# Two causal attentions: first placings between the first visits, warm-up products, and three dense products a step in the last unit

## The chip, the cores and the metric

One core of a Trainium2 chip runs one program. The metric is its time on the device in microseconds, the median of three runs. TensorE (PE) multiplies into PSUM; VectorE (DVE), ScalarE (ACT) and GpSimd (POOL) do the rest of the work, SyncE (SP) issues loads. TensorE runs at one of two clock levels, 1.2 and 2.4 GHz; the profile shows the granted share (0.50 or 1.00) of each stretch.

## The reference

Four layers on 1024 tokens of 256 features: in each an attention of some kind and then a feed-forward part. The change touches two attentions with 16 heads of dimension 16, one in layer 0 and one inside the feed-forward part of layer 1 (without bias and without rotation). Both are

```python
q = rope(proj(Wq, bq))
k = rope(proj(Wk, bk))
v = proj(Wv, bv)
attn = jnp.einsum('bhqd,bhkd->bhqk', q, k) * scale
causal = jnp.triu(jnp.ones((s, s), dtype=bool), k=1)
attn = jnp.where(causal, -jnp.inf, attn)
attn_weights = jax.nn.softmax(attn, axis=-1)
out = jnp.einsum('bhqk,bhkd->bhqd', attn_weights, v)
```

The layer's first line is `x = x + _L0_attn_ref(_layernorm(x, axis=-1), ...)`; the program runs the parts one after another, each in blocks that all engines enter and leave together.

## The kernel before

`small_attention` calls `project` (q, k and v), `attend_causal` and `out_product`. `attend_causal` is what changes. Its tensors carry the prefix `a0h_` in the first attention (about 57 to 278 us of the profile) and `a2h_` in the second (about 1531 to 1753 us).

The work is cut into 8 *units*: a quad of four heads (`Q` 0 to 3) times one half of the 512 queries (`h`), in the order Q0, Q1 for the first half, Q0, Q1 for the second, then Q2 and Q3 likewise. A unit has 4 or 8 *steps*, one for each 128 keys, 48 in all. Step `g` computes the scores of four heads transposed (keys by queries, `scores(g, 0)` and `scores(g, 1)`, L1227, in banks 2 to 4 by turns), ScalarE takes the exponential of each (L1333, `prob`), and `values(g - 1)` multiplies the step before with v into bank 5 (L1249). On the diagonal a mask is added by small bf16 products (L1164).

Ahead of a unit's steps its row maxima must be known. *Visits* (`A`, `maxima(x)`, L1192 and the mask, 48 of them) compute the scores the other way round, and VectorE reduces them (L1366). `M` (`max_rows`, L1211) turns a unit's maxima into rows with eight products, and VectorE adds them to the q tensor (`add_maxima`, L1384, `m_added`); `scores(g, 0)` of a unit's first step waits for that. *Placings* (`P`, `place(i, c)`, L1175 and L1176) spread the heads' 16 rows of q (c = 0) and k (c = 1) over partitions with the 0/1 matrix `put`; a placing is four products of 512 columns, and ScalarE rounds the result into `qt` or `kt` (`rounding`, L1315 and L1317). `D` and `R` are transposes for the denominators behind a unit (L1260, L1269); `ou` is a unit's result copied by ScalarE (L1345).

`A`, `M`, `P`, `D` and `R` share a ring of two PSUM pairs (`ring`, `spare`, `wait_spare`): the use number in `uses` picks the pair, and a use waits until the second last one was read. The order of all this is written out by hand: `head` comes ahead of the steps, `after[g]` lists what stands in step `g`, and `visits_by(g)` says how many visits are done by step `g`. On TensorE a step is

```python
scores(g, 0)
others(events[:1])
scores(g, 1)
events = events[1:]
others(events)
if 0 < g <= len(steps):
    values(g - 1)
others([e for e in after[g] if e[0] in "DR"])
```

Before the first placing VectorE clears `put` (L1353), GpSimd fills six pieces of it from the identity (L1147), then `one_row`, the masks and the negative identity (`made`), ScalarE makes the high part of the chunks of `qk` (`high`, L1305) and VectorE the low part (L1357). The head's order is: four placings, visits 0 to 3, four placings, `M` of unit 0, visits 4 and 5.

## Time and profile before

| | us |
|---|---|
| median of 3 runs | 2941.66 |
| lowest and highest run | 2924.04 and 2943.62 |
| profiled execution | 2920.74 |
| its span (the profile's) | 2919.0 |
| mean granted clock of TensorE | 0.911 |
| busy: PE, DVE, ACT, POOL | 2560.7, 1620.0, 1261.6, 1276.2 |

The profile gives the span of one execution. A busy TensorE is not TensorE at its peak, since matmuls overlap and their ends are modelled. A product whose operands are both plain fp32 stands there as two records. A line's number is a line of the kernel; `x8` behind a row is the number of instructions merged in it.

### The profile page before, as it was taken

The numbers are of one execution on the slowest core, as the hardware profiler recorded it, in microseconds if no ns is written. First come the engines' busy times: TensorE is split into PE (matmuls) and PEld (weight loads), VectorE is DVE, ScalarE is ACT, GpSimd is POOL, SyncE is SP. The second block draws the span as 40 slices with busy tenths as digits, with TensorE's granted clock in tenths as the row PEclk, the third lists the DMA queues.
The fourth block names the chain that finished last, engine by engine and source line by source line (L and its number), as shares of the span: only waits on it lengthen the run. The fifth ranks groups of instructions, "written<-read, shape, count | busy, mean of one in ns | idle before, by whom it ended". The sixth has DMA issues, their size and how long they took to land. (4 is left out here: it accounts for less than half of the span.)

```text
span 2919.0 us, 41072 instructions
## 1 busy us (share of the span) xinstructions
PE 2560.7 (88%) x14559; PEld 1710.4 (59%) x14562; DVE 1620.0 (55%) x2144; ACT 1261.6 (43%) x2127; POOL 1276.2 (44%) x1116
## 2 busy tenths in 40 slices
PE   5887799784999999999867886979999988997698
PEld 4443677562444444444554434768888866775576
DVE  3662355475666666664335543467777744554555
ACT  3464233371555555555323562245655542333232
POOL 3000344282888888888502002245454522442143
PEclk7696899996999999999975897989999997999799
DMA  1000111102111011010100001010000001110011
GB/s 48 1 1 8 36 44 49 45 24 81 37 35 37 23 37 37 15 30 1 29 11 5 1 1 41 19 56 19 26 30 19 19 4 34 49 44 19 24 44 41
DMA packets 40142, 82.17 MB, mean 28 GB/s; under 512 B 7856, under 2 KB 21424, under 8 KB 39472
## 3 DMA queue, kind: packets, MB, share of 16 engines
q1 hardware_dynamic: 37392, 76.25, 9.3%
q10 hardware_dynamic: 2592, 3.82, 0.4%
q8 instruction: 98, 1.61, 0.2%
q14 instruction: 60, 0.49, 0.1%
HBM read 60.12 MB, written 3.15 MB: 22 GB/s over the span
## 5 line engine op out<-in xcount | busy, mean ns | idle before, releaser
L1836 DVE TENSOR_REDUCE a1h_mseg<-bank 128x2 f32<-128x1024 f32 x256 | 302.4, 1222 | 185.0 <-PE bank L1601 176.8
L1763 ACT ACTIVATE a1h_prob<-bank 128x512 f32<-128x512 f32 x440 | 246.9, 598 | 189.9 <-PE bank L1657 103.1
L1585 POOL TENSOR_TENSOR a_qk<-a_qk,a1h_prob 128x512 f32<-128x512 f32 x230 | 298.7, 1330 | 48.9 <-ACT a1h_prob L1763 48.9
L63 POOL TENSOR_TENSOR f_wh<-f_raw,ones_r 128x768 fp32r<-128x768 f32 (+1 forms) x74 | 111.3, 1503 | 408.1 <-PE bank L402 371.2
L391 PE MATMUL bank<-x_norm_h,f_wh 128*128 128x512 f32 x592 | 241.6, 408 | 10.1 <-POOL f_wl L359 9.6
L391 PE MATMUL bank<-x_norm_l,f_wh 128*128 128x512 f32 x592 | 237.1, 401 | 0.0
L391 PE MATMUL bank<-x_norm_h,f_wl 128*128 128x512 f32 x592 | 236.5, 399 | 0.0
L600 DVE SCALAR_TENSOR_TENSOR f_tf<-bank,f_bias,f_sg 128x512 f32<-128x512 f32 x148 | 111.0, 751 | 201.6 <-PE bank L391 181.1
L1670 PE MATMUL bank<-a1h_prob,a_v 128*64 128x512 f32 x880 | 215.0, 603 | 0.0
L1655 PE MATMUL bank<-a1h_ql,a1h_k 128*128 128x512 f32 x512 | 202.1, 395 | 0.0
L488 ACT ACTIVATE f_hhi<-f_hf 128x512 fp32r<-128x512 f32 x124 | 78.3, 632 | 271.9 <-DVE f_hf L608 271.7
L614 DVE TENSOR_TENSOR f_hlo<-f_hf,f_hhi 128x512 fp32r<-128x512 f32 x124 | 112.1, 905 | 82.7 <-ACT f_hhi L488 82.4
L477 ACT ACTIVATE f_sg<-bank,f_bias 128x512 f32<-128x512 f32 x148 | 101.8, 688 | 128.1 <-PE bank L391 128.1
L1585 POOL TENSOR_TENSOR x_norm<-x_norm,a1h_prob 128x512 f32<-128x512 f32 x104 | 134.7, 1330 | 24.7 <-ACT a1h_prob L1763 24.6
L391 PEld LDWEIGHTS bank<-x_norm_h,f_wh 128*128 128x128 f32 x592 | 113.5, 192 | 52.0 <-issue 13.3
L359 POOL TENSOR_TENSOR f_wl<-f_raw,f_wh 128x768 fp32r<-128x768 f32 (+1 forms) x74 | 127.6, 1725 | 5.9
L402 PE MATMUL bank<-f_hhi,f_wh 128*128 128x512 f32 x296 | 118.4, 400 | 13.3 <-DVE f_hlo L614 13.3
L391 PEld LDWEIGHTS bank<-x_norm_l,f_wh 128*128 128x128 f32 x592 | 113.2, 191 | 27.8
L391 PEld LDWEIGHTS bank<-x_norm_h,f_wl 128*128 128x128 f32 x592 | 113.5, 192 | 24.8
L1654 PE MATMUL bank<-x_norm_h,a1h_kn 128*128 128x512 f32 x256 | 119.4, 467 | 4.1 <-DVE a1h_k L1824 2.2
L2616 POOL TENSOR_TENSOR l2a_rope<-l2a_rope,l2a_tab 128x512 f32<-128x512 f32 x64 | 81.2, 1276 | 90.1 <-ACT l2a_rope L2493 89.1
L1654 PE MATMUL bank<-x_norm_l,a1h_kn 128*128 128x512 f32 x256 | 118.5, 463 | 0.9
(564 smaller groups left out, 6189.8 us busy)
## 6 DMA issues: line engine op xcount, KB each, us to landing
f_raw<-in_l_w_dram SPq DMA_DIRECT2D x66, 385.0 KB, 3.1
a1h_st_q<-a_qk SPq DMA_DIRECT2D x128, 128.0 KB, 2.4
a_qk<-l_keys SPq DMA_DIRECT2D x32, 128.0 KB, 2.8
l2a_qkraw<-in_l2a_wqk_dram SPq DMA_DIRECT2D x32, 128.0 KB, 2.1
l2a_vraw<-in_l2a_wvg_dram SPq DMA_DIRECT2D x8, 512.0 KB, 3.8
f_raw<-in_l_w_dram SPq DMA_DIRECT2D x8, 449.0 KB, 3.4
a1p_raw<-in_l1a_w_dram SPq DMA_DIRECT2D x20, 128.0 KB, 2.0
l_keys<-a_qk SPq DMA_DIRECT2D x4, 512.0 KB, 4.0
```

The source lines that it names most:

```text
L63: return pool.tensor_tensor(dst, src, one.to_broadcast(list(src.shape)), ALU.mult)
L359: pool.tensor_tensor(wl[:, slot, :], raw[:, slot, 0:B], wh[:, slot, :].bitcast(F32), ALU.subtract).then_inc(w_split, 1)
L391: mm = pe.matmul(out[:, :], w[:, slot, c0:c0 + P], x, start=n == 0, stop=n == 3 * n_k - 1)
L402: mm = pe.matmul(acc[m][h][:, :], w[:, slot, c0:c0 + P], x[:, h, :], start=begin and n == 0, stop=False, skip_group_check=True)
L600: dve.scalar_tensor_tensor(tf[:, h, :], up[h][:, :], bias[:, slot, 1:2], sg[:, h, :], ALU.add, ALU.mult).then_inc(t_ready, 1)
L614: dve.tensor_tensor(hl[:, h, :], src[:, h, :], hh[:, h, :].bitcast(F32), ALU.subtract).then_inc(hl_ready, 1)
L1585: pool.tensor_tensor(out, first, slot_of[t % NP], ALU.add).then_inc(sum_done, 1)
L1654: pe.matmul(bank[:, :], kn[:, G % 2, a, keys], QA[n % 2][:, a, half(h)], start=True, stop=False)
L1655: mm = pe.matmul(bank[:, :], k1[:, a, keys], ql[:, n % 2, a, half(h)], start=False, stop=lo >= hi)
L1670: pe.matmul(core.bank[5][64 * a:64 * a + 64, :], v[:, kb, 2 * (n // 4) + a, :], slot_of[t % NP], start=kb == 0, stop=kb == TB - 1, skip_gr ...
L1763: act.activation(slot_of[t % NP], core.bank[2 + t % 3][:, :], ACT.Exp, scale=scale).then_inc(p_ready, 1)
L1836: dve.tensor_reduce(mseg[:, :, qb, s], spare(("A", n, k))[:, :, :], AX.X, ALU.max).then_inc(a_read, 1)
```

## The change

- The head becomes: four placings, then visits 0 to 3 with one of the other four placings behind each, then `M` of unit 0. Visits 4 and 5 leave the head and stand in step 0. `visits_by` is one visit lower at each step.
- All eight placings of the head (`FIRST`) leave the ring: they use the pairs 1 and 2 by turns (banks 2 to 5, of the scores and the values) and wait for `rounded` of the second last. A unit's first scores wait for `rounded` 8.
- GpSimd makes the first two kinds of `put` (three pieces), ScalarE the other two (three `Copy` activations, `keys_made`), behind the first two `high`. The first placing waits for three pieces, the next three for ScalarE's.
- Ahead of the first placing TensorE makes four products of the identity with a half of `qk` (plain fp32, 512 columns) into bank 5. Their result is not used.
- In visits 0 to 3 each pair of heads gets its mask (`mask_pair`) right behind its product; before, both pairs' masks came behind both products.
- In `after[g]` visits now come first, then `M` and `P`. So between the two score pairs of a step stands a visit where there is one, and `M` comes behind the second pair.
- `high` of chunks 2 and 3 moves from steps 0 and 1 to steps 8 and 9.
- In steps 40 to 47 TensorE makes three more products of 512 columns (`zero_r` with `kt`, fp32r, into bank 1) behind `values`. Their result is not used.

```diff
@@ -1043,12 +1043,11 @@
 
     def visits_by(g):
 
-        return min(len(visits), 6 + g + 1 + min(4, max(0, g - 1)))
+        return min(len(visits), (6, 7, 8, 10, 12, 14, 16)[g] if g < 7 else g + 10)
 
     after = [[] for _ in range(len(steps) + 6)]
-    head = [("A", x) for x in range(4)] + [("M", 0)] + [("A", x) for x in range(4, 6)]
     for g in range(len(steps)):
-        for x in range(visits_by(g - 1) if g else 6, visits_by(g)):
+        for x in range(visits_by(g - 1) if g else 4, visits_by(g)):
             after[g].append(("A", x))
             for w in range(1, len(UNITS)):
                 if LAST_VISIT[w] == x:
@@ -1056,19 +1055,23 @@
     for w in range(len(UNITS)):
         after[LAST_STEP[w] + 3].append(("D", w))
         after[LAST_STEP[w] + 5].append(("R", w))
-    head = [("P", i, c) for i in range(2) for c in range(2)] + head[:4]
-    head += [("P", i, c) for i in range(2, 4) for c in range(2)] + [("M", 0)] + [("A", x) for x in range(4, 6)]
+    head = [("P", i, c) for i in range(2) for c in range(2)]
+    for x in range(4):
+        head += [("A", x), ("P", 2 + x // 2, x % 2)]
+    head.append(("M", 0))
+    FIRST = [e for e in head if e[0] == "P"]
     for Q in range(2, QUADS):
         x = min(x for x, vi in enumerate(visits) if UNITS[vi[0]][0] == Q)
         first = min(g for g in range(len(steps)) if ("A", x) in after[g])
         for i in range(4):
             after[first - 3 + min(i, 2)].append(("P", 2 * Q + i // 2, i % 2))
     placed = [e for e in head if e[0] == "P"] + [e for es in after for e in es if e[0] == "P"]
-    after = [[e for e in es if e[0] in "APM"] + [e for e in es if e[0] in "DR"] for es in after]
+    after = [[e for k in ("A", "MP", "DR") for e in es if e[0] in k] for es in after]
     order = head + [e for es in after for e in es]
     uses = []
     for e in order:
-        uses += [("A", e[1], 0), ("A", e[1], 1)] if e[0] == "A" else [e]
+        if e not in FIRST:
+            uses += [("A", e[1], 0), ("A", e[1], 1)] if e[0] == "A" else [e]
     use = {e: u for u, e in enumerate(uses)}
 
     def width(g):
@@ -1082,7 +1085,8 @@
         sem = lambda n: nc.alloc_semaphore(f"{name}_{n}")
         sb = lambda n, shape, dt=F32: ctx.enter_context(nc.sbuf_tensor(f"{name}_{n}", shape, dt))
         c_in, made, hi, lo = sem("c_in"), sem("made"), sem("hi"), (sem("lo0"), sem("lo1"))
-        rounded, cleared = sem("rounded"), sem("cleared")
+        rounded, cleared, keys_made = sem("rounded"), sem("cleared"), sem("keys_made")
+        first_placed = sem("first_placed")
         a_ready, a_read, m_steps, m_added = sem("a_ready"), sem("a_read"), sem("m_steps"), sem("m_added")
         s_ready, p_ready, av_done = sem("s_ready"), sem("p_ready"), sem("av_done")
         ou_done, r_steps, rx_done, on_done = sem("ou"), sem("r_steps"), sem("rx"), sem("on")
@@ -1108,10 +1112,16 @@
 
         def spare(key):
 
+            if key in FIRST:
+                return core.pair[1 + FIRST.index(key) % 2]
             return ring[use[key] % 2]
 
         def wait_spare(pe, key):
 
+            if key in FIRST:
+                if FIRST.index(key) >= 2:
+                    pe.wait_ge(rounded, FIRST.index(key) - 1)
+                return
             u = use[key] - 2
             if u < 0:
                 return
@@ -1141,7 +1151,7 @@
         def _(pool):
             pool.wait_ge(cleared, 1)
             columns = core.ident[:, :].rearrange("p (n v u) -> p v u n", v=4, u=2)
-            for kind, places in enumerate(PLACES):
+            for kind, places in enumerate(PLACES[0:2]):
                 rows = put[:, kind, :, :].rearrange("p v (u n) -> p v u n", u=2)
                 for s in places:
                     pool.tensor_scalar(rows[:, :, :, 16 * s:16 * s + 16], columns, 1.0, None,
@@ -1175,7 +1185,7 @@
                     pe.matmul(ps[:, t, :], put[:, 2 * c, i % 4, :], HI[g][:, c, half(t)], start=True, stop=False)
                     mm = pe.matmul(ps[:, t, :], put[:, 2 * c + 1, i % 4, :], LO[g][:, c, half(t)], start=False,
                                    stop=True)
-                mm.then_inc(a_ready, 1)
+                mm.then_inc(first_placed if ("P", i, c) in FIRST else a_ready, 1)
 
             def maxima(x):
 
@@ -1194,13 +1204,19 @@
                                        tile_position=(64 * u, 0))
                     if not diag:
                         mm.then_inc(a_ready, 1)
-                if diag:
+                    elif x < 4:
+                        mask_pair(x, p, n)
+                if diag and x >= 4:
                     for p in range(2):
-                        ps = spare(("A", x, p))
-                        for c in range(2):
-                            for u in range(2):
-                                mm = mask(pe, ps[:, u, n - P + 64 * c:n - P + 64 * c + 64], 0, c, u)
-                        mm.then_inc(a_ready, 1)
+                        mask_pair(x, p, n)
+
+            def mask_pair(x, p, n):
+
+                ps = spare(("A", x, p))
+                for c in range(2):
+                    for u in range(2):
+                        mm = mask(pe, ps[:, u, n - P + 64 * c:n - P + 64 * c + 64], 0, c, u)
+                mm.then_inc(a_ready, 1)
 
             def max_rows(w):
 
@@ -1219,6 +1235,7 @@
                 c0, n, diag = width(g)
                 if kb == 0 and p == 0:
                     pe.wait_ge(m_added, w + 1)
+                    pe.wait_ge(rounded, len(FIRST))
                 if 4 * g + 2 * p >= 2:
                     pe.wait_ge(p_ready, 4 * g + 2 * p - 1)
                 for u in range(2):
@@ -1283,9 +1300,13 @@
                     else:
                         inverse(x)
 
-            pe.wait_ge(made, 7)
-            others(head[:4])
-            pe.wait_ge(made, 8)
+            for x in range(4):
+                pe.matmul(core.bank[5][:, :], core.ident[:, :], qk[:, 0, half(x % 2)], start=True, stop=True)
+            pe.wait_ge(made, 3)
+            others(head[:1])
+            pe.wait_ge(keys_made, 3)
+            others(head[1:4])
+            pe.wait_ge(made, 5)
             others(head[4:])
             for g in range(len(steps) + 6):
                 events = [e for e in after[g] if e[0] in "APM"]
@@ -1297,6 +1318,9 @@
                 others(events)
                 if 0 < g <= len(steps):
                     values(g - 1)
+                if LAST_STEP[-2] < g < len(steps):
+                    for _ in range(3):
+                        pe.matmul(ring[0][:, 1, :], core.zero_r[:, :], kt[:, 0, half(0)], start=True, stop=True)
                 others([e for e in after[g] if e[0] in "DR"])
 
         @block.scalar
@@ -1308,7 +1332,10 @@
                 Q = i // 2
                 if Q >= SLOTS and i % 2 == 0:
                     act.wait_ge(s_ready, 4 * (LAST_STEP[UNITS.index((Q - SLOTS, 1))] + 1))
-                act.wait_ge(a_ready, use["P", i, c] + 1)
+                if ("P", i, c) in FIRST:
+                    act.wait_ge(first_placed, FIRST.index(("P", i, c)) + 1)
+                else:
+                    act.wait_ge(a_ready, use["P", i, c] + 1)
                 dst = (qt, kt)[c][:, 2 * (Q % SLOTS) + i % 2, :]
                 src = spare(("P", i, c)).rearrange("p h q -> p (h q)")
                 if c == 0:
@@ -1318,7 +1345,13 @@
 
             high(0)
             high(1)
-            act.wait_ge(made, 7)
+            act.wait_ge(cleared, 1)
+            columns = core.ident[:, :].rearrange("p (n v u) -> p v u n", v=4, u=2)
+            for kind, places in enumerate(PLACES[2:4]):
+                rows = put[:, 2 + kind, :, :].rearrange("p v (u n) -> p v u n", u=2)
+                for s in places:
+                    act.activation(rows[:, :, :, 16 * s:16 * s + 16], columns, ACT.Copy).then_inc(keys_made, 1)
+            act.wait_ge(made, 4)
             for kind, i, *c in head:
                 if kind == "P":
                     rounding(i, c[0])
@@ -1332,8 +1365,8 @@
                         act.wait_ge(s_ready, t + 1)
                         act.activation(prob[:, t % NP, 0:n], core.bank[2 + t % 3][:, 0:n], ACT.Exp,
                                        scale=scale).then_inc(p_ready, 1)
-                if g < 2:
-                    high(g + 2)
+                if 8 <= g < 10:
+                    high(g - 6)
                 for e in after[g]:
                     if e[0] == "P":
                         rounding(e[1], e[2])
@@ -1370,7 +1403,7 @@
                     if w >= 2:
                         dve.wait_ge(m_added, w - 1)
                     elif w == 0:
-                        dve.wait_ge(made, 10)
+                        dve.wait_ge(made, 7)
                     out = mpos[:, w % 2, :, 48:P:64].rearrange("p (a b) u -> p a u b", a=2)
                     got = mseg[:, w % 2, :, :, :].rearrange("p (a u) b s -> p a u b s", a=2)
                     for p in range(2):
```

## Rows read from the trace of the kernel before

**Rows 1.** Windows: us, length; busy (count) of PE, PEld, DVE, ACT, POOL; PEclk; DMA.

```profile
57.50:90.20 32.70, 19.16 (x118) 13.21 (x118) 12.72 (x17) 11.61 (x12) 10.24 (x10) 0.73 0.04 11
90.20:132.70 42.50, 36.68 (x274) 19.51 (x276) 26.97 (x34) 15.02 (x36) 4.71 (x2) 0.58 0.00 1
132.70:241.40 108.70, 94.33 (x932) 47.68 (x930) 69.19 (x91) 69.59 (x146) 0.00 (x0) 0.99 0.00 1
241.40:272.70 31.30, 25.58 (x142) 8.85 (x142) 1.12 (x3) 15.77 (x35) 0.00 (x0) 0.53 0.01 1
...
1531.70:1566.60 34.90, 21.90 (x120) 15.52 (x120) 13.03 (x18) 11.80 (x12) 10.23 (x10) 0.63 0.04 10
1566.60:1609.80 43.20, 37.91 (x274) 20.06 (x276) 26.66 (x33) 15.13 (x37) 4.72 (x2) 0.54 0.00 1
1609.80:1723.30 113.50, 99.66 (x932) 50.43 (x928) 69.29 (x91) 69.59 (x147) 0.00 (x0) 0.93 0.01 1
1723.30:1747.90 24.60, 18.88 (x142) 6.81 (x142) 1.12 (x3) 15.70 (x35) 0.00 (x0) 0.79 0.00 1
```

**Rows 2.** Timeline, first head: start, us, engine, line, operation [idle before, releaser].

```profile
58.84 5.36 POOL L1147 TENSOR_SCALAR a0h_put<-ident 128x128 fp32r<-128x128 f32 x6 [8.04 <-DVE a0h_put L1353]
...
64.41 0.80 PE L1175 MATMUL bank<-x_norm_h,a0h_put 128*128 128x512 f32 x1 [7.68 <-POOL a0h_one_row L1149]
...
70.64 1.11 ACT L1317 ACTIVATE a0h_kt<-bank,a0h_one_row 128x1024 fp32r<-128x1024 f32 x1
...
71.85 0.44 PE L1192 MATMUL bank<-a0h_kt,a0h_qt 64*128 64x128 f32 x4 [1.25 <-ACT a0h_kt L1317]
...
72.40 0.76 DVE L1366 TENSOR_REDUCE a0h_mseg<-bank 128x2 f32<-128x256 f32 x2 [11.16 <-PE bank L1164]
...
73.71 1.29 DVE L1366 TENSOR_REDUCE a0h_mseg<-bank 128x2 f32<-128x512 f32 x2 [0.56 <-PE bank L1164]
...
78.47 2.36 DVE L1366 TENSOR_REDUCE a0h_mseg<-bank 128x2 f32<-128x1024 f32 x2 [1.02 <-PE bank L1164]
...
79.75 0.79 PE L1175 MATMUL bank<-x_norm_h,a0h_put 128*128 128x512 f32 x1 [1.21 <-DVE a0h_mseg L1366]
...
85.58 1.00 PE L1211 MATMUL bank<-a0h_nident,a0h_mpos 128*128 128x128 f32 x8
...
86.62 1.22 DVE L1384 TENSOR_TENSOR a0h_qt<-a0h_qt,bank 128x1024 fp32r<-128x1024 f32 x1 [5.51 <-PE bank L1211]
...
90.20 1.08 ACT L1333 ACTIVATE a0h_prob<-bank 128x512 f32<-128x512 f32 x2 [2.01 <-PE bank L1164]
```

**Rows 3.** Timeline of GpSimd alone, 60.5 to 62.3.

```profile
60.37 1.99 POOL L1147 TENSOR_SCALAR a0h_put<-ident 128x128 fp32r<-128x128 f32 x2
```

**Rows 4.** Timeline of TensorE's weight loads, 11.5 to 13, in the first norm.

```profile
11.86 0.19 PEld L128 LDWEIGHTS bank<-x_resid,mean_w 128*128 128x128 f32 x1 [0.24 <-issue]
12.29 0.19 PEld L128 LDWEIGHTS bank<-x_resid,mean_w 128*128 128x128 f32 x1 [0.24 <-issue]
```

**Rows 5.** Windows (columns as in rows 1) ahead of the first placing.

```profile
58.00:60.00 2.00, 0.00 (x0) 0.00 (x0) 2.00 (x3) 1.49 (x2) 1.16 (x1) 0.76 0.50 115
```

**Rows 6.** Timeline, first head again, two placing products at full clock.

```profile
83.16 0.40 PE L1175 MATMUL bank<-x_norm_h,a0h_put 128*128 128x512 f32 x1
...
83.40 0.39 PE L1176 MATMUL bank<-x_norm_l,a0h_put 128*128 128x512 f32 x1
```

**Rows 7.** Timeline of ScalarE, step 38 of the first attention.

```profile
238.47 0.66 ACT L1333 ACTIVATE a0h_prob<-bank 128x256 f32<-128x256 f32 x2 [1.87 <-PE bank L1164]
```

**Rows 8.** Timeline, step 44 of the second attention: the first scores of the step.

```profile
1737.37 0.49 PE L1227 MATMUL bank<-a2h_qt,a2h_kt 64*128 64x512 f32 x2
```

**Rows 9.** Timeline of ScalarE, last unit of the second attention.

```profile
1735.29 1.09 ACT L1333 ACTIVATE a2h_prob<-bank 128x512 f32<-128x512 f32 x2 [2.49 <-PE bank L1227]
...
1738.04 1.08 ACT L1333 ACTIVATE a2h_prob<-bank 128x512 f32<-128x512 f32 x2
...
1747.85 0.60 ACT L1345 ACTIVATE a2h_ou<-bank 128x512 f32<-128x512 f32 x1 [0.55 <-PE bank L1249]
```

## The prediction

> **What bounds the kernel now.** The granted clock comes first. Over the whole span its mean is 0.91, but the table of stretches [rows 1] shows where it is low, and two of the places are the two causal attentions that the change touches. I cut each into five stretches: the head (block start to the first exponential), steps 0 to 7, the middle (steps 8 to 39), the last unit (steps 40 to 47), and the end, which the change does not touch. The first attention spends 32.7, 42.5, 108.7 and 31.3 us, the second 34.9, 43.2, 113.5 and 24.6. So 431 of 2919 us can move and nothing else can. TensorE was busy 36.68 of 42.5 us in steps 0 to 7 at a clock of 0.58, and 94.33 of 108.7 us in the middle at 0.99. The last unit is the most telling pair: the same 142 records of TensorE took 31.3 us at a clock of 0.53 and 24.6 us at 0.79. There the visits have run out, TensorE alternates with ScalarE's exponentials, and the clock falls to its lower level (1.2 of 2.4 GHz).
>
> The timeline of the first head [rows 2] is a chain. GpSimd makes six pieces of the placing matrix; TensorE's first placing starts at 64.41, 6.9 us after the block began at 57.5; four placings and their roundings end at 71.75 (70.64 + 1.11); the first visit's product starts at 71.85 and the fourth visit's reduce ends at 80.83 (78.47 + 2.36); only from 79.75 do the other four placings run; the row maxima are added at 86.62, and the first exponential starts at 90.20, behind visits 4 and 5.
>
> **The head, part by part.** (a) GpSimd makes three of the six pieces before the first placing, ScalarE the other three. The six took 5.36 us [rows 2]; the first ran alone to 60.37, and the next two ended at 62.36 [rows 3]. The first placing moves from 64.41 to 62.4, 2.0 us earlier. ScalarE rounds the first two chunks of `qk` and then has nothing until a placing is ready; three copies of 128 columns, an eighth of the 1.1 us rounding's 1024 each, hide behind GpSimd (were each a whole rounding, they would end near 62.9 and still be in time for the second placing).
>
> (b) Four full fp32 products are put ahead on TensorE, which waits for nothing then. The nearest fp32 product is that of the mean, two records each; at the full clock their weight loads are 0.43 us apart [rows 4], so a product is 0.86 us and four are 3.4: 57.5 to 60.95, inside the wait. At half clock throughout they are 6.9 us and end at 64.4, where the placing starts today: even then they cost only what (a) gained. What they buy is the clock: without them it fell between 58 and 60 (0.76 in that stretch [rows 5]) with TensorE idle since the value products, and the first placings ran at half speed.
>
> (c) The four placings. At full clock their products are 0.24 us apart [rows 6], 0.96 for the four of one placing, so ScalarE's roundings (1.0 and 1.1 us) lead: 62.4 + 1.05 + four roundings of 1.1 each with their wait gives 67.8. At half clock it is 62.4 + 4 × 1.7 + 1.2 = 70.4. TensorE still idles 1.4 us between the products and the first placing, so I take 68.3.
>
> (d) Visits 0 to 3 with one placing behind each. Today 9.0 us from first product to last reduce, of which VectorE's four pairs of reduces are about 6.2 (0.76, 1.29, a pair between, 2.36) [rows 2]. The placings no longer use the ring of two PSUM pairs and go into TensorE's gaps, and each half of a visit now gets its mask directly. I leave 8.7 us for this, then the eight products of the row maxima (1.0), the addition (1.2), and 1.4 for scores and hand-overs: 12.3 us. The first exponential: 68.3 + 12.3 = 80.6, against 90.20: **-9.6**. The second attention's head has the same work and took 34.9 us [rows 1]; 23.1 us again gives **-11.8**. At half clock throughout, a placing is 1.7 us, a visit about 1.4, the row maxima 2: about 17 us from a start at 70.4, hence 87.4, gains of only 2.8 and 5.0.
>
> (e) Visits 4 and 5 are not gone. They now sit in step 0; the reduces of such a pair of visits are 0.76 and 1.29 [rows 2]: **+2.0** each attention (between 0 and the 2.5 of a slow clock).
>
> **The middle.** The count of visits done by each step falls by one, so each unit's row maxima (`M`) come in the last step of the unit before (units 1, 2, 3, 6, 7), behind that step's visit. Today `M` stands between the two score pairs of a step, and the exponentials then wait 1.87 us [rows 7]. That stall goes, but its place is taken: after `M` come the addition (1.2) and the first scores of the new unit, and where a 512-wide visit stands in front of it VectorE does 2.4 us of reduces first; `values` of that step covers 0.6 to 1 us. I count five boundaries at +0.4 and two freed steps at -0.5: **+1.0** each attention. The bounds: a full 1.9 us won at each of two freed steps (-4), or an addition and a 1.2 us half visit fully exposed at five (+12). Two 1.06 us roundings `high` move from steps 0 and 1 to 8 and 9; TensorE is the later one there about half of the time: **+0.8** (0 to 2.1). Later `P`s move by one step with their visits: nothing.
>
> **The last unit.** Three products of 512 columns a step in eight steps. At the full clock 0.7 us a step [rows 6]; at the lower 1.3. They stand between `values` and the next step's scores, and those follow one another without a gap in the stretch of the second attention's last unit that ran at full clock (values end, scores start at 1737.37 [rows 8]), so they are on the path: TensorE leads by 0.2 to 0.5 us there, and only the places with ScalarE's extra copies hide some. Without them, the unit at full clock is 2.75 us for a step (1735.29 to 1738.04) and 9.8 for the last four (1738.04 to 1747.85) [rows 9]: 4 × 2.75 + 0.7 for a transpose + 9.8 = 21.5. Eight times 0.7 less 0.6 hidden: 26.5. That is **-4.8** against 31.3 and **+1.9** against 24.6. It rests on the clock staying up: TensorE's share rises from about two thirds to four fifths. The Trainium skill ("TensorE: Matmul & The Clock Gate", section "Back-to-back issue gap") gives about 131 ns for a 512-column product in a real stream. By its figure the 48 products would cost 6.3 us instead of 11.3 (48 x 0.235), and the sum would come out 5 us lower, at 2920; the rows here show 0.24, and I keep them.
>
> **Sum.** First attention: -9.6 + 2.0 + 1.0 + 0.8 - 4.8 = -10.6. Second: -11.8 + 2.0 + 1.0 + 0.8 + 1.9 = -6.1. Together -16.7 us. Against the profiled execution, 2920.74 us, that is 2904; the three runs shown have a median of 2941.66, 21 us above it, so in their terms it is 2925.
>
> **Rivals.**
> 1. *The dense products do not lift the clock.* The last unit stays at the lower level and is PE-bound: 31.3 + 8 × 1.28 = 41.5 us in both, +10.2 and +16.9 instead of -4.8 and +1.9. Sum +13.3: 2955, slower than before. For it: at the lower level TensorE was already busy 25.58 of 31.3 us [rows 1] and the clock did not rise. Against: a packed 1.3 us a step closes most of what was idle. It decides when over half of the unit's steps run at 0.5. 10%.
> 2. *Steps 0 to 7 turn warm.* The head ends at the full clock; if it held, VectorE would lead with 27 us of reduces and additions (26.97 busy today [rows 1]) and the stretch would be near 33 instead of 42.5: 10 us less in each, 2905. Against: these steps have small products and long waits for reduces, and the clock fell there both times. 17%.
> 3. *The head stays cold*, because of the 1.4 us gap and thin visits: 6.8 us lost in each, 2939. 13%.
> 4. *The row maxima become the wait.* If at five boundaries in each attention the addition and half a visit (2.4 us) are exposed and the freed stalls give nothing: +24 - 2 = +22, 2947, again slower. It shows in exponentials waiting over 4 us at the first step of a unit. 10%.
>
> My forecast itself has 50%. The median of three runs of this kernel moves over 20 us (2924 to 2944), so about 1% is what can be told from no change. The range 2897 to 2950 takes in rivals 2, 3 and 4 and leaves out the first and the tails. Faster by over 1% (below 2912) is most of rival 2 and the low end of my own: 0.20. Slower by over 1% needs rivals 1 and 4 together: 0.04. Within 1%: 0.76.
>
> **What would show it.** First placing 4.9 us after the block start; four mean-like products ahead of it with a clock of 1.0; first exponential 23 us after the start (rival 3: 30); steps 0 to 7 near 44 us (rival 2: 33); no 1.87 us wait inside a step, but one of 2 to 3 us at the first step of units 3, 6 and 7; the last unit 26 to 27 us in both at a clock over 0.9 (rival 1: 41 at 0.5). The rest of the kernel, some 2490 us, must not move; if it does by more than 5 us, the difference isn't the change.

## The result and the profile after

| | before | changed kernel |
|---|---|---|
| median of 20 runs each, us | 2942.47 | 2925.01 |
| lowest and highest | 2918.15 and 2957.85 | 2916.04 and 2933.75 |
| ratio, 95% interval | | 0.9952 [0.9934, 0.9969] |
| profiled execution, us | 2920.74 | 2933.75 |

The changed kernel is 0.5% faster, within the 1% that was called no change, and lands on the 2925 that was forecast. Its runs lie closer together (18 us against 40).

The stretches of the two attentions, cut as in [rows 1] (start, length, busy time and count of PE, PEld, DVE, ACT, POOL, granted clock, DMA share, GB/s): head, steps 0 to 7, steps 8 to 39, last unit.

```profile
58.40:81.20 22.80, 17.55 (x104) 10.61 (x106) 11.37 (x14) 12.63 (x14) 8.41 (x7) 0.97 0.06 16
81.20:122.90 41.70, 34.84 (x288) 18.58 (x288) 27.47 (x34) 13.35 (x34) 0.00 (x0) 0.62 0.00 1
122.90:236.70 113.80, 99.94 (x944) 51.61 (x942) 70.38 (x93) 71.49 (x148) 4.75 (x2) 0.92 0.01 1
236.70:271.70 35.00, 29.72 (x166) 12.59 (x166) 1.12 (x3) 15.81 (x34) 0.00 (x0) 0.70 0.00 1
1535.60:1558.20 22.60, 17.32 (x104) 10.54 (x106) 11.42 (x14) 12.69 (x14) 8.41 (x7) 0.99 0.06 15
1558.20:1600.60 42.40, 35.06 (x290) 19.89 (x288) 27.43 (x34) 13.35 (x34) 0.00 (x0) 0.62 0.00 1
1600.60:1714.30 113.70, 99.68 (x944) 51.15 (x942) 70.38 (x93) 71.53 (x149) 4.74 (x2) 0.92 0.01 1
1714.30:1746.80 32.50, 27.25 (x166) 11.65 (x166) 1.11 (x3) 15.79 (x35) 0.00 (x0) 0.78 0.00 1
```

Against [rows 1]: the heads fell from 32.7 and 34.9 us to 22.8 and 22.6. Steps 0 to 7 stayed (42.5 and 43.2 to 41.7 and 42.4). The middle went from 108.7 to 113.8 in the first attention and stayed at 113.5 in the second. The last unit grew from 31.3 to 35.0 and from 24.6 to 32.5, with 24 more records of TensorE. With the transposes behind it an attention went from 220.1 and 221.0 us to 217.8 and 215.6.

So in these two executions the attentions gained 7.7 us, while the medians differ by 17.5. The profiled execution of the changed kernel is the slowest of its 20 runs. What lies outside the attentions, where nothing was changed, took 2478 us in the profiled execution of before and 2499 in that of the changed kernel; over all 14 profiled executions of this study it lies between these two values. The prediction said that the rest must not move by more than 5 us, or else the difference isn't the change. It moved by 21, so the spans of these two executions can't be compared; what follows goes by stretches and by medians. An execution of before that was profiled later (below) took 233.9 and 234.0 us for its attentions. The mean over both profiles of before is 227.3 an attention, and the changed kernel's 216.7 is 10.6 less: 21 us for the two. That is near the medians' difference, but it is an estimate: the two executions of before (2920.7 and 2959.2 us) lie near the two ends of its runs, there is one of the changed kernel, and what lies outside the attentions is left out of it. The first profile of before, on which the prediction rests, is of an execution near the fast end of its runs.

The head, in the timeline (compare [rows 2]):

```profile
58.34 3.67 PE L1304 MATMUL bank<-a_on,ident 128*128 128x512 f32 x8 [0.79 <-PEq L821]
...
59.67 3.52 POOL L1157 TENSOR_SCALAR a0h_put<-ident 128x128 fp32r<-128x128 f32 x3 [7.80 <-DVE a0h_put L1386]
...
60.24 1.08 ACT L1353 ACTIVATE a0h_put<-ident 128x128 fp32r<-128x128 f32 x3
...
63.25 0.50 PE L1185 MATMUL bank<-x_norm_h,a0h_put 128*128 128x512 f32 x1 [1.23 <-POOL a0h_put L1157]
...
63.59 0.39 PE L1186 MATMUL bank<-x_norm_l,a0h_put 128*128 128x512 f32 x1
...
63.82 0.39 PE L1185 MATMUL bank<-x_norm_h,a0h_put 128*128 128x512 f32 x1
...
67.87 1.11 ACT L1344 ACTIVATE a0h_kt<-bank,a0h_one_row 128x1024 fp32r<-128x1024 f32 x1
...
81.23 1.09 ACT L1366 ACTIVATE a0h_prob<-bank 128x512 f32<-128x512 f32 x2 [2.06 <-PE bank L1174]
```

The four fp32 products take 3.67 us and end at 62.0; GpSimd has three pieces to make, ScalarE's three take 1.08 us beside them. The first placing starts 4.9 us after the block start, with products 0.23 us apart as in [rows 6]; the last rounding of the first four ends at 68.98, the first exponential starts at 81.23, 22.9 us after the block start.

The row maxima of unit 7, in step 39:

```profile
231.19 0.33 PE L1244 MATMUL bank<-a0h_qt,a0h_kt 64*128 64x128 f32 x2
...
232.97 1.39 PE L1227 MATMUL bank<-a0h_nident,a0h_mpos 128*128 128x128 f32 x8 [1.38 <-DVE a0h_mpos L1410]
...
234.29 0.47 PE L1244 MATMUL bank<-a0h_qt,a0h_kt 64*128 64x128 f32 x2
...
234.40 1.22 DVE L1417 TENSOR_TENSOR a0h_qt<-a0h_qt,bank 128x1024 fp32r<-128x1024 f32 x1 [1.57 <-PE bank L1227]
...
234.99 0.45 ACT L1366 ACTIVATE a0h_prob<-bank 128x128 f32<-128x128 f32 x2 [2.86 <-PE bank L1174]
...
235.84 0.79 PE L1244 MATMUL bank<-a0h_qt,a0h_kt 64*128 64x512 f32 x2
```

TensorE's first score pair of step 39 ends at 231.5. All visits are done by step 38, so none stands in this step, and the one event that there is, `M`, comes between the two score pairs; behind the second pair it would stand only in a step with a visit. It waits for the last visit's reduces until 232.97 (1.38 us idle). The second pair follows at 234.29, and ScalarE's exponentials wait 2.86 us for it (2.66 in the second attention), where they waited 1.87 in step 38 before ([rows 7]). The addition runs from 234.40 and unit 7's first scores start at 235.84. The same place by windows:

```profile
231.00:233.00 2.00, 0.62 (x11) 0.34 (x7) 1.79 (x4) 0.67 (x3) 0.00 (x0) 1.00 0.00 0
233.00:235.00 2.00, 2.00 (x18) 1.79 (x22) 0.60 (x1) 0.01 (x1) 0.00 (x0) 0.65 0.03 8
235.00:237.00 2.00, 1.63 (x10) 0.31 (x6) 0.62 (x1) 0.71 (x3) 0.00 (x0) 0.50 0.00 0
```

The clock is at its upper level through the wait and falls at 233.6, within the second stretch (0.65), while the row maxima run. It stays at 0.50 for 24 us. In the second attention it falls at 1711.6, 0.9 us after the row maxima began, and stays low for 17 us. One step's dense products at each level, in TensorE's timeline:

```profile
242.53 1.93 PE L1266 MATMUL bank<-a0h_prob,a_v 128*32 128x512 f32 x8
244.39 1.65 PE L1323 MATMUL bank<-a0h_kt,zero_r 128*128 128x512 f32 x3
245.97 0.80 PE L1244 MATMUL bank<-a0h_qt,a0h_kt 64*128 64x512 f32 x2
...
263.67 1.07 PE L1266 MATMUL bank<-a0h_prob,a_v 128*32 128x512 f32 x8
264.66 0.96 PE L1323 MATMUL bank<-a0h_kt,zero_r 128*128 128x512 f32 x3
265.55 0.39 PE L1244 MATMUL bank<-a0h_qt,a0h_kt 64*128 64x256 f32 x2
```

At the lower level `values` start at 242.53, the three products at 244.39, and the next scores follow at 245.97: 1.58 us. At the upper level 264.66 to 265.55: 0.89 us.

### The profile page after: what moved, and what is told of

Read it like the earlier page. It is cut to its first block and busy times, and to the rows that moved or that the text cites. A ratio compares the mean times of both kernels' runs of the same rounds, so it can differ in the third digit from the quotient of the medians.

```text
span 2932.0 us, 41205 instructions
## 1 busy us (share of the span) xinstructions
PE 2584.7 (88%) x14626; PEld 1727.4 (59%) x14626; DVE 1621.4 (55%) x2144; ACT 1264.1 (43%) x2133; POOL 1273.0 (43%) x1110
## 5 line engine op out<-in xcount | busy, mean ns | idle before, releaser
L391 PEld LDWEIGHTS bank<-x_norm_h,f_wh 128*128 128x128 f32 x592 | 114.3, 193 | 52.1 <-issue 13.4
L391 PEld LDWEIGHTS bank<-x_norm_l,f_wh 128*128 128x128 f32 x592 | 114.3, 193 | 28.1
L1687 PE MATMUL bank<-x_norm_h,a1h_kn 128*128 128x512 f32 x256 | 119.4, 466 | 5.3 <-DVE a1h_k L1857 3.5
L1366 ACT ACTIVATE a0h_prob<-bank 128x512 f32<-128x512 f32 (+3 forms) x192 | 83.8, 489 | 85.3 <-PE bank L1174 56.4
```

The costliest lines, as they stand in the source:

```text
L391: mm = pe.matmul(out[:, :], w[:, slot, c0:c0 + P], x, start=n == 0, stop=n == 3 * n_k - 1)
L1687: pe.matmul(bank[:, :], kn[:, G % 2, a, keys], QA[n % 2][:, a, half(h)], start=True, stop=False)
```

## The experiments

Stretches of each kernel's profiled execution, first and second attention, in us. "Sum" is both attentions, including the transposes at the end.

| kernel | head | steps 0 to 7 | steps 8 to 39 | last unit | sum | median, us | ratio to before [95%] |
|---|---|---|---|---|---|---|---|
| before | 32.7, 34.8 | 42.5, 43.2 | 108.7, 113.5 | 31.2, 24.6 | 441.1 | 2942.5 | |
| before again | 34.8, 34.8 | 43.2, 43.2 | 119.4, 119.4 | 31.6, 31.6 | 467.9 | one run, 2959.2 | |
| changed | 22.9, 22.6 | 41.7, 42.4 | 113.8, 113.7 | 35.0, 32.5 | 433.4 | 2925.0 | 0.9952 [0.9934, 0.9969] |
| e1 no dense | 22.9, 22.6 | 41.4, 42.6 | 114.3, 113.7 | 23.0, 23.0 | 412.9 | 2913.8 | 0.9917 [0.9881, 0.9953] |
| e2 dense only | 32.7, 34.7 | 42.5, 43.2 | 111.5, 113.4 | 27.3, 29.9 | 444.2 | 2944.0 | 1.0014 [0.9985, 1.0042] |
| e3 no warm-up | 23.9, 24.1 | 42.8, 40.7 | 113.5, 114.3 | 30.5, 37.6 | 436.0 | 2929.9 | 0.9974 [0.9949, 0.9999] |
| e4 fill the wait | 22.5, 22.9 | 42.6, 43.2 | 114.8, 115.6 | 22.6, 23.9 | 416.7 | 2907.3 | 0.9894 [0.9846, 0.9943] |
| e5 old order | 22.5, 22.5 | 41.2, 41.2 | 116.3, 116.2 | 26.4, 26.4 | 420.9 | 2921.8 | 0.9940 [0.9907, 0.9973] |
| e6 visits earlier | 22.5, 22.5 | 45.6, 45.6 | 111.7, 111.8 | 27.5, 27.5 | 423.4 | 2907.1 | 0.9875 [0.9807, 0.9943] |
| e7 six dense | 22.9, 22.9 | 41.1, 41.7 | 112.9, 113.8 | 34.9, 36.8 | 435.0 | one run, 2925.6 | |
| e9 old head order | 25.8, 24.9 | 38.5, 43.1 | 114.4, 115.2 | 27.9, 26.4 | 424.6 | 2913.8 | 0.9961 [0.9937, 0.9985] |
| e10 fill all waits | 22.7, 22.9 | 45.7, 45.6 | 120.7, 116.4 | 23.9, 23.9 | 429.8 | 2917.9 | 0.9971 [0.9955, 0.9987] |
| e11 roundings early | 22.9, 22.8 | 41.4, 41.6 | 112.4, 112.9 | 24.9, 24.9 | 413.4 | 2908.2 | 0.9940 [0.9919, 0.9962] |
| e12 both | 22.5, 22.7 | 41.9, 44.1 | 112.8, 115.2 | 31.2, 28.1 | 427.6 | 2911.8 | 0.9921 [0.9897, 0.9944] |

Kernels of one group (e1 to e4; e5 to e7 and before again; e9 to e11; e12) ran on one chip each, against the kernel before on the same chip, whose median there was 2939.4, 2938.5, 2927.7 and 2936.6. Ratios can be compared across groups, medians less so.

**Without the dense products (e1).**

```diff
-                if LAST_STEP[-2] < g < len(steps):
-                    for _ in range(3):
-                        pe.matmul(ring[0][:, 1, :], core.zero_r[:, :], kt[:, 0, half(0)], start=True, stop=True)
```

> The changed kernel without the three products a step in the last unit; everything else stays. In the changed kernel the last unit took 35.0 and 32.5 us. Theory A (the clock falls because the row maxima M7 now wait for a visit's reduce directly before the unit, with TensorE idle; the dense products only lengthen each step, 1.4 us at the lower clock and 0.9 at the higher): the clock still falls ahead of the last unit, its low steps take 4.1 us again instead of 5.7, and the unit takes 29 to 33 us if the clock stays low, 25 to 27 if it comes back in the middle; the kernel is 2 to 12 us faster than the changed one. Theory B (the dense products pay, because they alone bring the clock back in the unit): the unit stays low to its end and takes over 33 us, and the kernel is slower than the changed one.

Windows of the two last units:

```profile
237.30:260.30 23.00, 17.54 (x142) 6.43 (x142) 1.11 (x3) 15.67 (x34) 0.00 (x0) 0.85 0.01 1
1704.90:1728.00 23.10, 17.55 (x142) 6.42 (x142) 1.12 (x3) 15.72 (x35) 0.00 (x0) 0.85 0.00 1
```

Where the clock came back in the first (windows, and TensorE's `values` behind them):

```profile
243.00:244.30 1.30, 1.30 (x6) 0.29 (x2) 0.00 (x0) 0.01 (x1) 0.00 (x0) 0.50 0.00 0
244.30:246.00 1.70, 0.95 (x8) 0.34 (x10) 0.00 (x0) 1.33 (x3) 0.00 (x0) 1.00 0.00 0
...
245.59 1.07 PE L1266 MATMUL bank<-a0h_prob,a_v 128*32 128x512 f32 x8
```

23.0 and 23.0 us, below every figure that either theory gave. The clock fell at 237.5 in the first attention, as the unit began, and 3 us ahead of the unit in the second, so theory A's place for it is about right. It came back after 7 and 10 us, without dense products. What brought it back isn't shown. By the ratios e1 gains 0.35% (10 us) more than the changed kernel, though the two intervals overlap at their ends; in the profiles the two attentions are 20.5 us shorter. Theory B falls: the clock comes back without the dense products. Against before, e1 is 0.83% faster: that is what all of the change but the dense products is worth.

**Only the dense products (e2).** The same three lines added to the kernel before.

> The kernel before with only the three dense products a step in steps 40 to 47 added; M7 stays one step earlier, in step 38. Before: 31.2 and 24.6 us. Theory A (where M7 stands decides on the clock; dense products then hold it): with M7 in its old place the dense products keep the clock up and the unit takes 26 to 27 us in both, the kernel 0 to 4 us faster than before. Theory B (the clock falls at the thin last steps of unit 6 anyway and dense products are too few to bring it back soon): 32 to 38 us in both, the kernel 5 to 15 us slower than before.

```profile
245.70:273.00 27.30, 22.00 (x166) 9.96 (x166) 1.11 (x3) 15.81 (x35) 0.00 (x0) 1.00 0.01 2
1727.90:1757.80 29.90, 24.65 (x166) 10.86 (x166) 1.12 (x3) 15.78 (x35) 0.00 (x0) 0.89 0.00 1
```

In the first attention the unit ran wholly at the upper level and took 27.3 us; this is the one execution in which the forecast's condition held, and there its 26.5 is nearly right. In the second the clock was low for 7 us at the unit's start: 29.9. Theory A nearly holds for the first (it said 26 to 27), neither for the second. The kernel as a whole isn't to be told from before (1.0014). The dense products don't keep the clock from falling. And even where it stayed up, 27.3 us is more than the 23.0 to 24.9 that the unit took without the products in e1 and e11, with the clock low for 7 to 12 of them: at 0.9 us a step the products cost more than the clock they were to save.

**Without the warm-up products (e3).**

```diff
-            for x in range(4):
-                pe.matmul(core.bank[5][:, :], core.ident[:, :], qk[:, 0, half(x % 2)], start=True, stop=True)
```

> The changed kernel without the four fp32 products ahead of the first placing. Heads in the changed kernel: 22.9 and 22.6 us at a clock of 0.97 and 0.99. Theory A (the clock in the head is theirs): the clock falls before the first placing, the placings run at 0.43 us a product instead of 0.24, and the heads take 26 to 30 us; the kernel is 6 to 14 us slower than the changed one. Theory B (the new order with placings between visits does it alone, the chain of roundings and reduces leads at either clock): the heads take 23 to 25 us and the kernel is within 4 us of the changed one.

Window of the first head:

```profile
58.70:82.60 23.90, 14.99 (x98) 10.23 (x98) 11.38 (x14) 12.64 (x14) 8.39 (x7) 0.86 0.06 15
```

and of its timeline, the first three products of a placing:

```profile
63.56 0.79 PE L1185 MATMUL bank<-x_norm_h,a0h_put 128*128 128x512 f32 x1 [5.68 <-POOL a0h_put L1157]
64.15 0.63 PE L1186 MATMUL bank<-x_norm_l,a0h_put 128*128 128x512 f32 x1
64.57 0.63 PE L1185 MATMUL bank<-x_norm_h,a0h_put 128*128 128x512 f32 x1
```

The clock is low at the first placing (products 0.42 us apart), as theory A says, and the head's mean clock falls from 0.97 to 0.86. But the head takes 23.9 us (24.1 in the second), 1.0 and 1.5 more than with them. Theory B's figure for the heads holds: in these profiles the four products are worth 2.5 us of the 22 that the two heads gained. Only the first placings ran slowly here: the clock was back at 66.8, 3 us after the first of them began. So what a head costs that stays cold throughout isn't shown. The median is 5 us higher than the changed kernel's, but the two intervals overlap; the last units (30.5 and 37.6) together took only 0.6 us more.

**Fill the wait ahead of the row maxima (e4).** e1, and in `max_rows`:

```diff
                 wait_spare(pe, ("M", w))
-                pe.wait_ge(m_steps, w + 1)
                 ps = spare(("M", w))
+                if w >= 6:
+                    for _ in range(6):
+                        pe.matmul(ps[:, 1, :], core.zero_r[:, :], kt[:, 0, half(0)], start=True, stop=True)
+                pe.wait_ge(m_steps, w + 1)
```

> The changed kernel without the dense products of the steps, but with six products of 512 columns in the wait for the reduces ahead of the row maxima of units 6 and 7 (into the PSUM pair that those use next). Theory A (the idle time of TensorE ahead of M7 is what lowers the clock): the clock stays at its upper level through unit 6's start and into unit 7, the six products (1.4 us) hide in the wait, and the last unit takes 21.5 to 25 us; the kernel is 8 to 16 us faster than the changed one. Theory B (thin scores and values lower it a few steps later anyway): the clock falls within unit 7 and it takes 27 to 31 us, no more than 5 us from the run without dense products.

```profile
237.00:259.60 22.60, 16.74 (x142) 6.17 (x142) 1.12 (x3) 15.58 (x34) 0.00 (x0) 0.92 0.00 1
1700.90:1724.80 23.90, 17.96 (x142) 6.48 (x142) 1.12 (x3) 15.62 (x35) 0.00 (x0) 0.86 0.00 0
```

and of its timeline, the fill in step 39 and the row maxima behind it:

```profile
232.56 1.66 PE L1227 MATMUL bank<-a0h_kt,zero_r 128*128 128x512 f32 x6
234.06 1.00 PE L1230 MATMUL bank<-a0h_nident,a0h_mpos 128*128 128x128 f32 x8
```

Six products fit the wait: step 39 took 4.24 us, against 4.28 and 5.05 in e1. The clock still fell, 3 to 4 us after the unit's first exponential, for 3 and 7 us (e1: with that exponential and 3 us ahead of it). 22.6 and 23.9 us are in theory A's range, yet e1 without the fill has 23.0 and 23.0. At unit 6 the fill didn't fit: step 31 took 6.28 against 5.18 and 5.93. So the idle wait isn't the cause by itself. Theory B's cause, the thin steps around it, fits but wasn't tested by itself. The ratio (0.9894) isn't separated from e1's (0.9917).

**The old order in a step (e5).** e1 with `after` sorted as before, `M` ahead of the visit.

```diff
-    after = [[e for k in ("A", "MP", "DR") for e in es if e[0] in k] for es in after]
+    after = [[e for e in es if e[0] in "APM"] + [e for e in es if e[0] in "DR"] for es in after]
```

> The changed kernel without the dense products and with the old order inside a step (the row maxima ahead of the visit, between the two score pairs). Reference is the same kernel with the new order: middle (steps 8 to 39) 114.3 and 113.7 us, 2914 us. Theory A (the wait for the reduces is the same wherever the row maxima stand, it only moves): middle 112 to 117 us in both, the kernel within 5 us. Theory B (the new order is what made the middle longer than before's 108.7 and 113.5, since the visit's half reduce and the addition now lie ahead of the unit's first scores): middle under 110 us in both, 8 us or more faster.

The middle took 116.3 and 116.2 us, 2.0 and 2.5 more than in e1, and steps 0 to 7 41.2. Its clock was 0.90 there against 0.93 and 0.92, so the 2 us can be the clock's and not the order's. Theory A holds for the middle, B falls: the new order isn't what makes the middle longer than 108.7. Its ratio, 0.9940, overlaps e1's, though the medians are 8 us apart on different chips.

**A visit earlier (e6).** e1 with the old `visits_by`.

```diff
-        return min(len(visits), (6, 7, 8, 10, 12, 14, 16)[g] if g < 7 else g + 10)
+        return min(len(visits), 6 + g + 1 + min(4, max(0, g - 1)))
```

> The changed kernel without the dense products and with one visit more done by each step, as before (three visits in step 0), so that the row maxima come a step earlier. Theory A (row maxima directly ahead of their unit are the cause of the 5 us step before units 3, 6 and 7 and of the clock falling there): the middle shrinks by 3 to 6 us in each attention, step 0 grows by 2 us, the kernel is 2 to 8 us faster than 2914. Theory B (each unit pays one wait of about 3 us anyway, wherever it stands): the middle stays within 2 us, steps 0 to 7 too, and the kernel within 3 us of 2914.

```profile
79.90:125.40 45.50, 39.43 (x298) 21.69 (x298) 28.38 (x36) 13.33 (x34) 0.00 (x0) 0.54 0.00 1
125.40:237.20 111.80, 100.58 (x932) 50.87 (x930) 69.39 (x91) 71.59 (x149) 4.73 (x2) 0.91 0.01 1
237.20:264.70 27.50, 21.59 (x142) 7.43 (x142) 1.11 (x3) 15.70 (x35) 0.00 (x0) 0.69 0.00 1
```

The middle shrank by 2.6 and 1.9 us (theory A said 3 to 6). Steps 0 to 7 grew by 3 to 4; step 0 alone, with one visit more and the clock low in both kernels, took 5.3 us instead of 3.1, the 2 that A said. And the last unit began without a wait (steps 38 and 39 5.5 us together instead of 6.5 to 7.3), but the clock fell in it all the same, 3 us after its start. In the profile the sum is 10 us worse than e1's; in the medians it is the best ratio, 0.9875, of only four runs (the profiled one is the slowest of them) and with an interval that holds e1's ratio. It isn't settled by these runs which is better.

**Six dense products a step (e7).** The changed kernel with `range(6)` for `range(3)`.

> The changed kernel with six dense products a step instead of three in the last unit. It prices one product and tells whether more of them hold the clock. Theory A (they lie on the path, 0.30 us each at the upper clock, 0.53 at the lower, and do not decide when the clock falls, because it falls ahead of them): steps at the upper clock take 2.75 + 1.8 = 4.5 us and 2.10 + 1.8 = 3.9, the last unit 38 to 46 us. Theory B (three are too few, six fill TensorE and bring the clock back within a few us): the low stretch in the unit is under 7 us in both attentions and the unit takes under 37 us.

```profile
236.60:271.40 34.80, 29.57 (x190) 15.49 (x190) 1.11 (x3) 15.77 (x34) 0.00 (x0) 0.92 0.00 1
1712.80:1749.70 36.90, 31.55 (x190) 16.18 (x190) 1.11 (x3) 15.85 (x35) 0.00 (x0) 0.86 0.00 0
```

and of its timeline, step 46:

```profile
266.04 1.65 PE L1323 MATMUL bank<-a0h_kt,zero_r 128*128 128x512 f32 x6
```

Steps 45 and 46 took 4.12 and 3.68 us where the changed kernel took 3.43 and 3.00 and e1 2.54 and 2.10. So the first three cost 0.90 us and the next three 0.69: 0.23 us for a product and 0.2 once a step. The clock was low for 7 us around the first unit's start and 14 us around the second's; neither theory's figures fit throughout. With three products the low stretches were 24 and 17 us here but 0 and 7 in e2, so one execution doesn't show that six shorten them; the units took 34.9 and 36.8 us against 35.0 and 32.5.

**The kernel before once more (e8).**

> The kernel before once more, unchanged, for a second profile. In the first its last units took 31.2 and 24.6 us and its heads 32.7 and 34.8. Theory A (the stretches of the attentions repeat within 1 us except where the clock's turns fall otherwise: steps 0 to 7, the last unit): heads again 32 to 35 us, the last units anywhere from 23 to 32. Theory B (each stretch has its own fixed time): all ten stretches within 1 us of the first profile.

Windows of its first attention:

```profile
59.30:94.00 34.70, 21.77 (x120) 15.45 (x120) 12.94 (x18) 11.68 (x11) 10.25 (x10) 0.62 0.04 10
94.00:137.20 43.20, 37.90 (x274) 20.05 (x276) 26.74 (x33) 15.14 (x36) 4.75 (x2) 0.54 0.00 1
137.20:256.70 119.50, 106.69 (x932) 53.44 (x930) 69.49 (x91) 69.84 (x147) 0.00 (x0) 0.86 0.01 1
256.70:288.30 31.60, 26.15 (x142) 9.03 (x142) 1.12 (x3) 15.79 (x35) 0.00 (x0) 0.50 0.00 1
```

The middle took 119.5 us at a clock of 0.86, where the first profile has 108.7 at 0.99 ([rows 1]); the last unit ran wholly at 0.50. Both attentions took 234 us. Theory A is right in kind but too narrow: the middle isn't fixed either.

**The second placings behind the visits again (e9).** e1, with

```diff
-    for x in range(4):
-        head += [("A", x), ("P", 2 + x // 2, x % 2)]
+    head += [("A", x) for x in range(4)] + [("P", 2 + x // 2, x % 2) for x in range(4)]
```

> The changed kernel without the dense products, and with the head's second four placings behind visits 0 to 3 again instead of between them; they still use the scores' banks, three pieces still come from ScalarE, the four fp32 products stay. Heads of the same kernel with the new order: 22.9 and 22.6 us. Theory A (the placings between the visits are the largest part of the 10 to 12 us that the head gained: they took 5.7 us behind the visits, of which half was hidden): the heads take 25.5 to 28 us and the kernel is 5 to 10 us slower than 2914. Theory B (leaving the ring is enough, since the placings then run while VectorE still reduces visit 3): the heads take 23 to 25 us, the kernel within 4 us.

```profile
59.60:85.40 25.80, 20.70 (x106) 13.39 (x106) 11.40 (x14) 12.55 (x14) 8.39 (x7) 0.80 0.05 14
1526.90:1551.80 24.90, 19.85 (x106) 12.35 (x106) 11.42 (x14) 12.71 (x15) 8.40 (x7) 0.86 0.05 14
```

25.8 and 24.9 us: 2.9 and 2.3 more. Theory A's range holds the first; the second lies in theory B's. The clock fell within these heads (to 0.80 and 0.86, against 0.98 and 0.99 in e1), so a part of the 2.9 and 2.3 is the clock's, and the two aren't taken apart. The interleaving is the largest single part of the head that was tried, of two. Steps 0 to 2 came out 3 us shorter in the first attention and 1 in the second; in the first the clock was up there, in e1 it was down.

**Fill all waits (e10).** e4 with the fill at units 1 to 7 (four products at 1 and 2).

> Dense products of 512 columns, with an unused result, in TensorE's wait ahead of the row maxima of every unit but the first (four for units 1 and 2, six for 3 to 7), and none in the steps of the last unit. With the fill at units 6 and 7 alone the last units took 22.6 and 23.9 us, the middle 114.8 and 115.6, steps 0 to 7 42.6 and 43.2, the kernel 2907. Theory A (each low stretch begins in such a wait, so filling it keeps the clock): the middle drops to 105 to 110 us at a clock over 0.96, steps 0 to 7 to 36 to 41, the kernel to 2885 to 2900. Theory B (low stretches come from the thin steps around too, and the fill costs where it does not fit the wait): each stretch stays within 2 us or grows, and the kernel is at 2905 to 2920.

Against e1, steps 0 to 7 grew by 3 to 4 us and the middle by 3 to 6. The middle's clock was 0.93 and 0.97 (e1: 0.93 and 0.92), that of steps 0 to 7 0.60 and 0.65 (0.64 and 0.58). Theory B. In steps 3, 7, 15, 19 and 23 the wait is shorter than the fill, and the dense products stand on the path.

**The two roundings early (e11).** e1 with `high` back in steps 0 and 1.

```diff
-                if 8 <= g < 10:
-                    high(g - 6)
+                if g < 2:
+                    high(g + 2)
```

> The changed kernel without the dense products and with the two roundings of the second half of qk back in steps 0 and 1 (from 8 and 9). Theory A (ScalarE is the later engine there about half of the time, as forecast: they cost 0.8 us an attention at steps 8 and 9): steps 8 and 9 together take 0.5 to 2 us less, steps 0 and 1 at most 0.5 more, the kernel 0 to 4 us faster than 2914. Theory B (TensorE leads in steps 8 and 9, the move cost nothing): steps 8 and 9 within 0.3 us of the same steps at the same clock level.

Steps 8 and 9 took 6.39 and 6.94 us instead of 6.82 and 7.17; steps 0 and 1 took 7.76 and 7.77 in both kernels. So the move costs 0.2 to 0.4 us an attention in these executions, between the two theories. The clock of steps 8 and 9 was lower in e11 than in e1 (0.73 against 1.00, 0.60 against 0.67), so it can be more.

**The combination (e12).** e11 with the fill of e4 at unit 7 alone.

> The changed kernel without the dense products of the steps, with the two roundings of the second half of qk in steps 0 and 1, and with six dense products in the wait ahead of the row maxima of unit 7 alone. Theory A (only the fill that fits its wait pays; it delays the clock's fall into the last unit): steps 38 and 39 stay at 2.3 and 4.3 us, the last units take 22.5 to 25 us, the middle 112 to 114, the attentions 203 to 208 each, the kernel 2900 to 2910 and 0.7 to 1.3% below before. Theory B (when the clock turns is chance, the fill does nothing): the last units anywhere between 23 and 28 us and the kernel within 4 us of 2908 to 2914.

```profile
234.40:265.60 31.20, 25.34 (x142) 8.79 (x142) 1.12 (x3) 15.69 (x34) 0.00 (x0) 0.54 0.00 1
```

The fill fitted (steps 38 and 39: 2.25 and 4.23 us), and the clock fell 2 us into the unit and stayed low to its end in the first attention: 31.2 us. With the same fill ahead of the same unit it was low for 3 and 7 us in e4. Theory A's range is missed; B's range for the last units is too (31.2 and 28.1), its median is met. Of the versions tried, e1, e4, e6 and e12 are all faster than before by 0.8 to 1.25%, and e1 is the plainest: the changed kernel without the step's dense products.

## Why the prediction was right, and where it wasn't

**The head: right in size, partly in cause.** Forecast -9.6 and -11.8 us, measured -9.8 and -12.2 (-11.9 and -12.2 against before again). The first placing came 4.9 us after the block start as forecast. Step (b), that the four products buy the clock, is right about the clock (0.97 instead of 0.86), and without them the heads took 1.0 to 1.5 us more (e3). The rival of a cold head (30 us) asked for the lower level throughout; that occurred in no run, so its size stays untested. Interleaving gives at most 2.3 to 2.9. The rest, some 6 to 8 us, lies with the earlier first placing, visits 4 and 5 behind the first exponential, the placings outside the ring, and the masks; these were not taken apart.

**Steps 0 to 7: wrong by 3 us an attention.** Forecast +2.0 for the two visits, measured -0.8 and -0.8. To price a visit by its reduces fits (e6's third visit in step 0 has 1.82 us of them and costs 2.1). The count doesn't: `visits_by` passes one visit on into the middle, so steps 0 to 7 have 13 visits instead of 12, one more and not two. In the second attention's timeline VectorE's reduces went from 24.0 to 25.4 us there, and from 58.8 to 59.7 in the middle, for which the forecast put nothing. What took back the rest isn't shown; a part can be the clock, which went from 0.58 and 0.54 to 0.62, that is, 4 and 8 us less at the lower level. Rival 2 (these steps turn warm) did not occur.

**The middle: not to be told.** Forecast +1.8 (+1.0 and +0.8), measured +5.1 and +0.2 against one execution of before and -5.7 against the other. Its parts have prices of one execution each: the row maxima a step later cost 1.9 to 2.6 (e6), the old order took 2 us more than the new at a lower clock (e5), and the two roundings cost 0.2 to 0.4 us (e11), where 0.8 was put. The difference between 108.7 and 119.4 in one unchanged kernel is the clock's (0.99 and 0.86). Of the signs, the wait inside a step did not go but grew (2.86 us in step 39); the waits at the first step were 2.7 us at unit 3, 4.1 to 4.4 at unit 6 and 1.3 at unit 7, and 5.7 and 6.6 at unit 1. So rival 4's sign (over 4 us) did show, though not its price. Where both kernels ran at the upper level, steps 36 to 39 took 11.5 us before and 12.4 in e1.

**The last unit: the step that failed.** Forecast 26.5 us in both; measured 35.0 and 32.5, together 14.5 us more. Two terms. The price of three products at the upper level was put at 0.7 us a step and is 0.9, as e7 shows: 0.23 each, which the rows gave, and 0.2 once. The one unit that ran wholly at the upper level (e2) took 27.3, 0.8 above the forecast. By that, some 13 of the 14.5 us are the other term, the condition "it rests on the clock staying up". It did not: the clock fell as the row maxima of unit 7 ran, and with the dense products in them the low steps took 5.7 us instead of 4.1 (1.58 a step for the products, where 1.3 was put). Why it falls there stays open. The wait that the change moved to this place isn't the cause by itself: the clock also fell in this unit or just ahead of it in all four attentions of before, with `M` a step earlier, and it fell in e4, e10 and e12, where the wait was filled. Rival 1 named the mechanism, products that don't hold the clock, and was given 10%; it held for 21 of the 35 us (to 257.4) and 14 of the 32, not for over half of the steps, and the units came out 3.7 and 7.9 us longer than before instead of its 10.2 and 16.9. The Trainium skill's figure ("TensorE: Matmul & The Clock Gate", section "Back-to-back issue gap", about 131 ns for a 512-column product in a stream) doesn't fit here: 0.23 us at the upper level.

**The sum.** -16.7 was forecast. The medians differ by 17.5. That the two agree this closely is luck: the last units cost 14.5 us more than forecast, and against that stands that the execution on which the terms were built was about 21 us faster than before's median, so that a typical execution of before had more to give. (A part of the 21 lies outside the attentions: 2478 us there, 2490 in before again.) With the mean of the two profiles of before in its place, the parts are -23.0 for the heads (34.8 is the head of three of four), -2.0 for steps 0 to 7, -3.0 for the middle, +8.0 for the last units and -1.1 behind them: -21 us. What the change brings is the head; what the dense products take back is about 10 us by e1's ratio, and 20 us by its one profile.

**Range and chances.** Within 1% had 0.76 and came true. The range of 53 us had to cover the clock's turns and the unknown terms; runs of before alone cover 40 us.

## What to carry to other kernels

Price filler products at both clock levels before adding them, and put them only where TensorE waits anyway, if at all: in that place (e4, e12) they cost nothing, but no gain from them is shown either; a filler on the path costs 1.8 times as much at the lower level, exactly when it was meant to help. When a forecast rests on the clock staying up, look in the rows at whether it ever did in that stretch: in before's last units it didn't. And when the clock turns differently from execution to execution, one profile of before is one draw: compare stretches over several profiles, or rest the verdict on medians.

## What the runs showed of the hardware that was not expected

- An unchanged stretch (the middle) took 108.7, 113.5 and 119.4 us in one kernel, at clocks of 0.99, 0.93 and 0.86. In before again both attentions, 1492 us apart, had the same lengths to 0.1 us in every stretch; so had e6, and e5 to 0.2 us. In each of these three the clock's first fall came equally long after the block start in both attentions, to 0.1 us (1.8 us in before again, 22.4 in e5, 22.5 in e6). In the changed kernel it came after 21.6 and 22.3 us, and the last units differ by 2.5 us. So the clock's turns repeat where they start alike; these few executions show no more than that.
- In 27 of the 28 profiled attentions the clock was at its lower level in some part of the last unit. With three dense products a step that part was 21, 14, 0, 7, 9 and 27 us (changed kernel, e2, e3), without them anything from 3 to 32 us. So these runs show neither that the products shorten it nor that they lengthen it; in the changed kernel the clock stayed at 0.50 for 24 us with dense products in every step.
- A burst of dense products behind another kind of product costs 0.2 us beyond their spacing (0.90 us for three, 1.59 for six).
